# Five of twelve chunks turned by DMA through one two-part buffer, with the row statistics moved on VectorE and GpSimd, in a two-layer graph attention kernel

## What is computed

```python
def _L0_gnn_ref(xx_anchor, input, adj, weight):
    anchor_adj = jnp.einsum('md,de,ne->mn', xx_anchor, weight, input)
    scores = jnp.where(adj > 0, anchor_adj, NEG_PAD)
    atten = jax.nn.softmax(scores / TEMPERATURE, axis=1)
    return atten @ input
def _L1_gnn_ref(mole_out, adj, W, a1, a2):
    Wh = mole_out @ W
    e = jax.nn.leaky_relu((Wh @ a1)[:, None] + (Wh @ a2)[None, :], negative_slope=ALPHA)
    att = jax.nn.softmax(jnp.where(adj > 0, e, NEG_INF), axis=1)
    return jax.nn.elu(att @ Wh)
x = _layernorm(x + _L0_gnn_ref(x, L0_gnn_input, adj, L0_gnn_weight), axis=-1)
x = _layernorm(x + _L1_gnn_ref(x, adj, L1_gnn_W, L1_gnn_a1, L1_gnn_a2), axis=-1)
```

## Time and profile before

| what | value |
| --- | --- |
| median of 3 runs | 1454.98 us (1452.93 to 1455.09) |
| profiled execution, its own time | 1453.21 us |
| its span | 1451.4 us |
| mean granted TensorE clock | 0.989 |
| busy: PE, PE weight loads | 1412.1 us (97%), 1010.3 us (70%) |
| busy: DVE, ACT, POOL | 1256.5 us (87%), 1070.0 us (74%), 1215.0 us (84%) |
| DMA queue q1 | 73.1% of 16 engines' span |

### The profile page before, as it was taken

One profiled execution on the slowest core, in us unless ns is written; L12 is line 12 of the kernel. 1 busy time (PEld: TensorE's weight loads), 2 busy tenths in 40 slices (PEclk: granted clock), 3 DMA queues, 4 the chain that ended last, 5 costly groups with the idle time before them and its releaser, 6 DMA issues.

```text
span 1451.4 us, 28334 instructions
## 1 busy us (share of the span) xinstructions
PE 1412.1 (97%) x9661; PEld 1010.3 (70%) x9661; DVE 1256.5 (87%) x2129; ACT 1070.0 (74%) x2437; POOL 1215.0 (84%) x904
## 2 busy tenths in 40 slices
PE   8899999999999999999999999979999999999995
PEld 4577777777777777777777777755666666666664
DVE  6999999999999899999999999839898898979794
ACT  6788888888888888888888888868655555545453
POOL 6788888888888888888888878738999999999995
PEclk9999999999999999999999999998999999999998
DMA  8999999999999999999999999663434344434320
GB/s 265 292 270 269 262 265 257 258 275 270 270 267 263 259 264 258 273 271 271 273 258 259 262 255 274 182 138 73 102 66 111 77 102 87 102 71 105 78 58 14
DMA packets 427918, 291.38 MB, mean 201 GB/s; under 512 B 356864, under 2 KB 403200, under 8 KB 427776
## 3 DMA queue, kind: packets, MB, share of 16 engines
q1 hardware_dynamic: 427776, 289.59, 73.1%
HBM read 160.56 MB, written 40.89 MB: 139 GB/s over the span
## 4 chain that ended last, share of the span: by engine, by line
PE 94%; DVE 3%; issue 1%; ACT 1%; POOL 0%; DMA 0%; ACTq 0%; DVEq 0%; SPq 0%; POOLq 0%
PE ps L617 17%; PE ps L703 13%; PE ps L696 12%; PE ps L643 11%; PE ps L619 9%; PE ps L656 8%; PE ps L655 8%; PE ps L654 8%; PE ps L680 6%; PE ps L587 1%; PE ps L714 1%; DVE rows L969 1%; DVE neg_mask L944 1%; PE ps L580 0%; DVE pT_lo L978 0%
## 5 line engine op out<-in xcount | busy, mean ns | idle before, releaser
L826 ACT ACTIVATE rows<-rows,exp_bias 128x512 f32<-128x512 f32 x576 | 416.8, 724 | 57.0 <-DVE exp_bias L1022 57.0
L528 POOL TENSOR_TENSOR p_lo<-p,p_hi 128x1024 fp32r<-128x1024 f32 x180 | 423.7, 2394 | 22.0 <-ACT p_hi L864 11.5
L969 DVE CUSTOM_DVE_ANT_0 rows<-ps,neg_mask 128x1024 f32<-128x1024 f32 x288 | 352.1, 1223 | 80.2 <-PE ps L656 72.8
L1049 DVE SCALAR_TENSOR_TENSOR p<-ps,e_col,edgesT 128x1024 f32<-128x1024 f32 x288 | 349.7, 1275 | 53.3 <-PE ps L673 36.7
L438 POOL TENSOR_SCALAR edges<-neg_mask 128x1536 uint8<-128x1536 bf16 x190 | 307.3, 1618 | 97.0 <-DVE neg_mask L944 85.1
L864 ACT CAST p_hi<-p 128x1024 fp32r<-128x1024 f32 x180 | 185.1, 1047 | 167.0 <-DVE p L1049 164.4
L617 PE MATMUL ps<-vals,pT_hi 128*128 128x256 f16 x1536 | 295.3, 273 | 1.4 <-ACT att L805 0.9
L812 ACT CAST pT_hi<-ps 128x512 f16<-128x512 f32 x384 | 222.7, 580 | 90.6 <-PE ps L643 90.4
L480 POOL TENSOR_TENSOR inp_sb<-rows,inp_sb 128x512 f16<-128x512 f32 x192 | 281.5, 1484 | 9.6 <-ACT inp_sb L820 1.9
L619 PE MATMUL ps<-vals,pT_lo 128*128 128x128 f16 x1536 | 274.6, 219 | 0.0
L978 DVE TENSOR_TENSOR pT_lo<-ps,pT_hi 128x512 f16<-128x512 f32 x384 | 250.8, 683 | 10.6 <-ACT pT_hi L812 10.6
(11 more groups left out here) (111 smaller groups left out, 1855.9 us busy)
## 6 DMA issues: line engine op xcount, KB each, us to landing
adj_sb<-adj SPq DMA_DIRECT2D x192, 768.0 KB, 5.6
edge_rows<-edges SPq DMA_DIRECT2D x192, 192.0 KB, 4.8
xq<-x SPq DMA_DIRECT2D x48, 64.0 KB, 2.9
xr<-x SPq DMA_DIRECT2D x48, 64.0 KB, 5.6
out<-y_w SPq DMA_DIRECT2D x5, 512.0 KB, 3.7
inp_sb<-inp SPq DMA_DIRECT2D x3, 768.0 KB, 8.2
inp_sb<-inp_sb SPq DMA_TRANSPOSE x96, 4.6
edgesT<-edge_rows SPq DMA_TRANSPOSE x48, 5.3
```

The source lines that it names most:

```text
L528: nc.gpsimd.tensor_tensor(p1_lo[:, m % LO_SLOTS, :], p1[:, (NB * g + n) % P_SLOTS, :], p1_hi[:, m % HI_SLOTS, :].bitcast(F32), ALU.subtrac ...
L826: nc.scalar.activation(row_chunk(1 - par, c), row_chunk(1 - par, c), ACT.Exp, bias=exp_bias[:, 1 - par:2 - par], scale=EXP_SCALE, accum_ou ...
L969: nc.vector.tensor_tensor_reduce(row_pair(par, k), scores_pair(k), neg_mask_row[:, 2 * k * CHUNK:2 * (k + 1) * CHUNK], 1.0, -3.0e38, ALU.a ...
L1049: nc.vector.scalar_tensor_tensor(out=p1[:, (NB * g + n) % P_SLOTS, :], in0=ps[:, R_ROW:R_ROW + 2, :].rearrange("p b w -> p (b w)"), scalar ...
```

## The change

- MOVED is 5 instead of 4: a fifth chunk goes by DMA, so PE turns seven chunks per tile instead of eight. ATT_STEP is 10 instead of 9, since it is counted from MOVED.
- `movedT` is one buffer instead of two, in two parts of three and two chunks (MOVED_PARTS). SP issues four transposing DMAs per tile instead of two, and each part waits until PE has used the same part of the tile before (`pv_done`). ACT's and POOL's waits on `movedT_in` go by part.
- The row statistics of tile t - 3 now stand in iteration t on DVE, at the head of c = 2 (STATS_STEP), where they were those of tile t - 2 at c = 11. On POOL the power, normalization and `s_prod` of tile t - 3 stand behind `moved_low(t - 1, 0)` of iteration t; the two additions of tile t - 2 stay at the iteration's end. ACT's sums go to c = 9 (SUMS_STEP).
- POOL no longer keeps `x1_total`. DVE sums the first 44 tiles in eight pieces in iteration 48, and PE adds the last four in `mean_of_wh`, with one column of `averager` instead of 128.
- The last tile: DVE makes the additions, the normalization and the two row sums (with `tensor_tensor_reduce`); only the power stays on POOL.

The diff, without the renaming of PSUM places and semaphores that follow from this:

```diff
@@ before L12 @@
 PV_LAG = 2
-MOVED = 4
+MOVED = 5
+MOVED_PARTS = ((0, 3), (3, 5))
 PARTS = 8
@@ before L97 @@
 moved_hi, moved_lo = (inp_space[:, i * MW:(i + 1) * MW] for i in range(2))
-movedT = inp_space[:, 2 * MW:6 * MW].rearrange("p (s h b m) -> p s h b m", s=2, h=2, m=P)
+movedT = inp_space[:, 2 * MW:4 * MW].rearrange("p (h b m) -> p h b m", h=2, m=P)
 xq = sb0("xq", [P, P], F32)
...
@@ before L276 @@
 ATT_STEP = LAG + PV_LAG + MOVED
+STATS_STEP, SUMS_STEP = 2, 9
+TOTALLED, TOTAL_PARTS = NB - 4, 8
 
@@ before L292 @@
 def movedT_loads(tile):
-    return 32 * (tile // 2 + 1)
+    return 32 * (tile + 1)
+
+def moved_part(i):
+    return next(k for k, (a, b) in enumerate(MOVED_PARTS) if a <= i < b)
 
@@ before L375 @@
             sp.wait_ge(moved_hi_set, MOVED * (tile + 1))
-            if tile < 2:
-                sp.wait_ge(vals_lo, MOVED * (tile + 2))
-            after(sp, pv_done, C * (tile - 1))
-            sp.dma_start_transpose(movedT[:, par, 0], moved_hi).then_inc(movedT_in[par], 16)
-            sp.wait_ge(moved_lo_set, MOVED * (tile + 1))
-            sp.dma_start_transpose(movedT[:, par, 1], moved_lo).then_inc(movedT_in[par], 16)
+            if tile == 0:
+                sp.wait_ge(vals_lo, 2 * MOVED)
+            for k, (a, b) in enumerate(MOVED_PARTS):
+                after(sp, pv_done, C * (tile - 1) + (C - MOVED) + b if tile >= 1 else 0)
+                for half, of, ready in ((0, moved_hi, moved_hi_set), (1, moved_lo, moved_lo_set)):
+                    sp.wait_ge(ready, MOVED * tile + b)
+                    sp.dma_start_transpose(movedT[:, half, a * BPC:b * BPC, :], of[:, a * CHUNK:b * CHUNK]
+                                           ).then_inc(movedT_in[k], 16)
         if t == NB + 1:
@@ before L467 @@
                                 ALU.mult).then_inc(s_prod_set, 1)
-        if j == 0:
-            nc.gpsimd.tensor_copy(x1_total[:], x1).then_inc(total_set, 1)
-        else:
-            pool.wait_ge(total_set, j)
-            nc.gpsimd.tensor_tensor(x1_total[:], x1_total[:], x1, ALU.add).then_inc(total_set, 1)
 
@@ before L478 @@
         if tile >= 1:
-            pool.wait_ge(movedT_in[(tile - 1) % 2], movedT_loads(tile - 1))
+            pool.wait_ge(movedT_in[moved_part(i)], movedT_loads(tile - 1))
         nc.gpsimd.tensor_tensor(moved_lo[:, i * CHUNK:(i + 1) * CHUNK], row_chunk(tile % 2, i),
@@ before L482 @@
 
+    def rstd_of_tile(tile):
+        pool.wait_ge(ve_set, tile + 1)
+        nc.gpsimd.tensor_tensor(small[:, 4:5], small[:, 3:4], consts[:, 0:1], ALU.pow).then_inc(rstd_set, 1)
+
     def tile_rstd(t, par, known):
@@ before L489 @@
             moved_low(t - 1, 0)
+        if t >= 3:
+            tile = t - 3
+            rstd_of_tile(tile)
+            pool.wait_ge(rstd_set, tile + 1)
+            nc.gpsimd.tensor_scalar(x1_all[:, tile, :], xr[:, 1 - par, :], moments[:, 0:1], small[:, 4:5], ALU.subtract,
+                                    ALU.mult).then_inc(x1_set, 1)
+            score_cols(tile)
+        if moved:
             moved_low(t - 1, 1)
@@ before L502 @@
                 vals_low(9)
+        if moved:
+            moved_low(t - 1, 4)
+        if ahead:
             make_edges(t + 1, 1)
@@ before L506 @@
             vals_low(11)
-        if ends_tile(known):
+        if 2 <= t <= NB:
             tile = t - 2
@@ before L513 @@
             nc.gpsimd.tensor_tensor(xr[:, par, :], att[:, P:2 * P], xr[:, par, :], ALU.add).then_inc(u_set, 1)
-            pool.wait_ge(ve_set, tile + 1)
-            nc.gpsimd.tensor_tensor(small[:, 4:5], small[:, 3:4], consts[:, 0:1], ALU.pow).then_inc(rstd_set, 1)
-            pool.wait_ge(rstd_set, tile + 1)
-            nc.gpsimd.tensor_scalar(x1_all[:, tile, :], xr[:, par, :], moments[:, 0:1], small[:, 4:5], ALU.subtract,
-                                    ALU.mult).then_inc(x1_set, 1)
-            score_cols(tile)
 
     tiles(pool, tile_rstd)
+    rstd_of_tile(NB - 1)
 
...
@@ before L717 @@
     def mean_of_wh():
-        pe.wait_ge(total_set, NB)
-        nc.tensor.matmul(ps[:, SPARE, 0:P], x1_total[:], averager[:], start=True, stop=True).then_inc(mean_turned, 1)
+        pe.wait_ge(total_set, TOTAL_PARTS)
+        nc.tensor.matmul(mean_ps, x1_total[:], averager[:, 0:1], start=True, stop=False)
+        pe.wait_ge(x1_set, NB)
+        for j in range(TOTALLED, NB):
+            mm = nc.tensor.matmul(mean_ps, x1_all[:, j, :], averager[:, 0:1], start=False, stop=(j == NB - 1))
+        mm.then_inc(mean_turned, 1)
         pe.wait_ge(mean_repd, 1)
-        nc.tensor.matmul(ps[:, SPARE, P:2 * P], mean_rep[:], w1_c[:, 0:P], start=True, stop=True).then_inc(mean_made, 1)
+        nc.tensor.matmul(ps[:, OUT3, P:2 * P], mean_rep[:], w1_c[:, 0:P], start=True, stop=True).then_inc(mean_made, 1)
 
...
@@ before L830 @@
                 xT_high(t + 1, 1 - par)
-            if c == 4 and t >= 3:
+            if c == SUMS_STEP and t >= 3:
                 score_sums(t - 3)
-            if c == C - 1 and t == NB + 1:
-                score_sums(t - 2)
 
@@ before L934 @@
 
+    def row_statistics(tile):
+        dve.wait_ge(u_set, tile + 1)
+        after(dve, x1_set, tile)
+        nc.vector.bn_stats(stats[:], xr[:, tile % 2, :]).then_inc(stats_set, 1)
+        dve.wait_ge(stats_set, tile + 1)
+        nc.vector.bn_aggr(moments[:], stats[:]).then_inc(moments_set, 1)
+        dve.wait_ge(moments_set, tile + 1)
+        nc.vector.tensor_scalar(small[:, 3:4], moments[:, 1:2], EPS, None, ALU.add).then_inc(ve_set, 1)
+
     def make_mask(t, q, known):
@@ before L953 @@
         for c in range(C):
+            if c == STATS_STEP and t >= 3:
+                row_statistics(t - 3)
             if known == 0:
@@ before L980 @@
 
+            if t == NB and 1 <= c <= TOTAL_PARTS:
+                d = slice((c - 1) * P // TOTAL_PARTS, c * P // TOTAL_PARTS)
+                dve.wait_ge(x1_set, TOTALLED)
+                nc.vector.reduce_sum(x1_total[:, d], x1_all[:, 0:TOTALLED, d].rearrange("p n d -> p d n"),
+                                     AX_X).then_inc(total_set, 1)
+
             if known == 0:
@@ before L1005 @@
                                             ALU.mult).then_inc(scaled_set, 1)
-                if c == ATT_STEP + 2:
-                    dve.wait_ge(u_set, t - 1)
-                    after(dve, x1_set, t - 2)
-                    nc.vector.bn_stats(stats[:], xr[:, par, :]).then_inc(stats_set, 1)
-                    dve.wait_ge(stats_set, t - 1)
-                    nc.vector.bn_aggr(moments[:], stats[:]).then_inc(moments_set, 1)
-                if c == ATT_STEP + 2:
-                    dve.wait_ge(moments_set, t - 1)
-                    nc.vector.tensor_scalar(small[:, 3:4], moments[:, 1:2], EPS, None, ALU.add).then_inc(ve_set, 1)
+                if c == ATT_STEP + 1 and t == NB + 1:
+                    dve.wait_ge(att_out, NB)
+                    dve.wait_ge(xr_in[par], 16 * (t // 2))
+                    nc.vector.tensor_tensor(xr[:, par, :], att[:, 0:P], xr[:, par, :], ALU.add).then_inc(u1_set, 1)
+                    dve.wait_ge(u1_set, NB)
+                    nc.vector.tensor_tensor(xr[:, par, :], att[:, P:2 * P], xr[:, par, :], ALU.add).then_inc(u_set, 1)
             if c == C - 1 and scores_of(known):
@@ before L1026 @@
 
-    dve.wait_ge(s_set, NB)
+    row_statistics(NB - 1)
+    dve.wait_ge(rstd_set, NB)
+    nc.vector.tensor_scalar(x1_all[:, NB - 1, :], xr[:, (NB - 1) % 2, :], moments[:, 0:1], small[:, 4:5], ALU.subtract,
+                            ALU.mult).then_inc(x1_set, 1)
+    dve.wait_ge(x1_set, NB)
+    dve.wait_ge(s_set, NB - 1)
+    for k in range(2):
+        nc.vector.tensor_tensor_reduce(s_prod[:, k, :], x1_all[:, NB - 1, :], wa_rep[:, k, :], 1.0, 0.0, ALU.mult,
+                                       ALU.add, s_cols[:, k, NB - 1:NB]).then_inc(s_last_set, 1)
+    dve.wait_ge(s_last_set, 2)
     nc.vector.reduce_max(s_top[:, 0:1], s_cols[:, 0, :], AX_X).then_inc(s_part, 1)
...
```

18 lines of the change are left out of this document (10 added, 8 removed).

## The result

The changed kernel takes 1488.78 us (median of 4 runs, 1483.09 to 1491.58) against 1453.95 us for the kernel before, run beside it: a ratio of 1.0238, 95% interval 1.0222 to 1.0255, or +34.8 us. It is slower, as forecast, but by 23 us more than forecast, and outside the range. The profiled execution took 1489.73 us, with a span of 1487.6 us and a granted clock of 0.988.

A forecast was written before the change was run, and what follows sets the result against it. PE bounds the kernel at 19.35 us per tile; the change closes a POOL-DVE loop of 19.63 us. 1453.2 + 12.6 - 0.9 - 1.8 + 1.0 = 1464.1 us, as a median 1466 us; range 1432 to 1480 us.

The forecast's parts named there:

- The part that saves: PE: one chunk per tile fewer to turn, 0.44 us, period 19.35 to 18.91 us if PE stays the bound.
- POOL's chain and the loop: POOL's quarter-2 edges to second addition, 17.29 us, plus 2.34 us back through DVE's statistics and mask: 19.63 us per tile.
- What would show it: Signs in the trace: quarter-2 mask wait 2.2 to 2.5 us, DVE idle before statistics, PE idle 0.5 to 0.9 us.
- The hold-up of 0.74 us per mask: POOL's instructions beside DVE's masks: three masks cost POOL 2.21 us per chain, 0.74 us each.
- The single buffer and the queue of SP: SP's four transposing DMAs and the loads queued with them: cost 0, up to +0.3 us per tile.
- They are used a period later, so nothing again: SP: two adj quarters and an edge store queue behind the later xr load; costed at nothing.
- Cost 0, up to +0.3 us per tile: SP: quarter 0 of adj, issued later; if it lands 1 us late, DVE's 1.8 us free time absorbs it.
- The end of the first layer: From ACT's last att to the maximum of row sums: -1.8 us, between -1 and -2.5.
- The reductions: DVE's eight reductions in iteration 48, 0.4 to 0.9 us each: +1.0 us taken, between 0 and +5.
- PE stays the bound: Rival: the loop closes below PE's 18.91 us per tile, giving 1433 us; chance 22%.
- Every mask blocks POOL for its whole length: Rival on POOL: the loop grows 0.6 us to 20.3 us, giving 1494 us; chance 7%.
- the DMA engines become the bound: Rival: a fifth chunk's transposes take DMA work from 18.4 to 20.2 us, giving 1492 us; chance 9%.

The follow-up runs named there:

- e7: e3 with ACT's row sums at c = 11 instead of c = 9 (timing only): 1437.51 us, ratio 0.9888.
- e2: The changed kernel with quarter 3 of adj loaded in only 192 of 1536 columns from tile 1 on (timing only): 1469.62 us, ratio 1.0115.
- e10: The changed kernel with statistics at c = 3, row sums at c = 11 and xr loaded behind quarter 3 of adj: 1453.57 us, ratio 1.0003.
- e12: The changed kernel with xr loaded behind quarter 3 of adj instead of behind quarter 1: 1473.21 us, ratio 1.0139.
- e3: The changed kernel with statistics at c = 3 and quarter 3 of adj loaded in 192 of 1536 columns (timing only): 1443.96 us, ratio 0.9930.
- e11: e10 with the next tile's small load xq issued ahead of the transposing DMAs: 1444.68 us, ratio 0.9942.
- e9: e10 with quarter 0 of the next tile's adj issued ahead of the transposing DMAs: 1491.81 us, ratio 1.0253.
- e8: e4 with xr loaded behind quarter 3 of adj instead of behind quarter 1: 1454.97 us, ratio 1.0008.
- e4: The changed kernel with four chunks by DMA instead of five, parts of two and two: 1467.29 us, ratio 1.0089.

## Why the prediction was wrong in size, point by point

**The part that saves: right.** 18.91 us per tile if PE is the bound: e7 has it.

**POOL's chain and the loop: right.** 17.29 us forecast, 17.37 in the trace; way back 2.34 and 2.36; period 19.63 and 19.73. "What would show it" asked for a wait of 2.2 to 2.5 us for the quarter-2 mask (2.36) and POOL near 84% busy (16.52 of 19.73 us, 84%). Its 0.10 us too little, times 45, is 4.5 us. That the chain came so near is partly luck: its masks cost 0.26 us less than put, and its five low parts 0.37 us more, since one that stands by itself takes up to 1.25 us to the next start and not 1.12. The statistics' idle time released by the second addition was to be there in nearly every tile; it is in 26 of 43 tiles (100 to 960 us), and in 43 once the load is light (e2): in the others `adj` had already delayed DVE.

**The hold-up of 0.74 us per mask: near, 0.65.** In the chain shown above it falls on a low part (1.75 against 1.16), the normalization (1.57 against 0.80) and an edge conversion (2.06 against 1.47): 1.95 us for three, 0.65 each. The Trainium skill's rule (SBUF — State Buffer, Who interferes with whom), that a 2-port VectorE instruction which is issued first blocks GpSimd for its whole length, would have made it 0.95 us each and the tile 20.3 us, by the rival that I drew from it; in steady tiles the trace doesn't agree in size, as POOL lost 0.59 to 0.77 us and the tile takes 19.73. The power on one column loses the same, 0.77 us: it takes 1.33 us in some tiles, 0.56 in others. In kind the trace agrees: in e10, as shown, whichever of mask and edge conversion starts first keeps its length and the other is held, the mask by 1.1 us.

**The single buffer and the queue of SP: this step failed.** "They are used a period later, so nothing again" looked at the quarters that queue behind `xr` and asked only whether they themselves would be late. They weren't. But by leaving 5 to 6 us late they are in flight beside the transposing DMAs. The "issues of some 2 us each" were right as a median (2.14 us); four of them hold SP for a median of 8.6 us, up to 10.1, where it is 7.1 with `xr` late (e12). Behind them `xq` and quarter 0 wait.

Two things failed in the treatment of quarter 0. The room was too small: the prediction had it issued 18.4 us into POOL's chain and wanted at 23.9 us, 5.5 us apart; in the tile shown it was issued at 18.8 us (523.97 - 505.15) and wanted at 23.4 us (528.57), 4.6 us apart, with a median of 4.4 us against a landing of 5.0. And that DVE's free time of 1.8 us "takes it up" was wrong: the time free per period is not free at a place on the loop. ACT's wait for the transposing DMAs and PE's for `xq` were put at nothing as well. "Cost 0, up to +0.3 us per tile": measured 20.21 - 19.73 = 0.48 us per tile as a mean, 21 us in all, of which `xr` alone is some 15 us (e12).

**The row sums at c = 9: not costed.** 0.19 us per tile where PE is the bound (e3 to e7), hidden behind the loop in the change as it stands.

**The end of the first layer: right, -1.9 for -1.8. The reductions: +0.8 for +1.0, by luck.** Each was put at 0.4 to 0.9 us and took 1.33 to 1.39, so 10.9 us of DVE's time went in and the `att` moved by 0.8. The second layer's +1.2 us was put at next to nothing; no run takes it apart.

The sum with the measured sizes: 45 x (19.73 - 19.35) - 0.9 - 1.9 + 0.8 + 1.2 = +16.3 us, beside +15.3 measured without the late loads (e2), and +21 for these: +37.3, beside 1489.73 - 1453.21 = +36.5 us between the profiled executions.

**The rivals.** "PE stays the bound" needed a loop under 18.91; it isn't. "Every mask blocks POOL for its whole length" and "the DMA engines become the bound" gave 1494 and 1492 us, near the result, by mechanisms that the runs don't bear out as put: no steady 20.2 or 20.3 us per tile, but 29 periods of 44 at the loop's 19.5 to 19.9 and the rest late in steps, and with another order on SP the same five chunks run at 18.91 in most tiles (e10, e11). The second was the nearer one, as the place is right: DVE waiting for `adj` before its masks was its sign, and it came. I gave it 9%. What I should have done is to price a partial form of it, a tile in three that is 1 to 3 us late. That the total fell near these two rivals' prices says nothing for their mechanisms.

**What stays open.** Why the load of some tiles lands a few tenths of a us later than that of their neighbours; where the step of 2.2 us comes from (that of 1.25 us goes with the order of mask and edge conversion in e10, untested by a run of its own); why `xq` ahead helped; and whether the slow transposing DMAs are held by the issuing side or by the engines that move the data. No run takes these apart. Two quarters of `adj` ahead of the transposing DMAs weren't tried, once one had cost what it did in e9.

## What to carry to other kernels

When a step moves the thing that a load in an ordered queue waits for, look at everything behind it in the queue, and ask not only whether it lands in time but what it will be in flight beside. An engine's free time per period is worth nothing at a place that lies on a loop through another engine: close the loop on paper, then add every wait that can fall on it. And a fifth chunk by DMA paid only once statistics, row sums and two small loads stood in the right places; the change and e11, the same code in two orders, are 44 us apart.

## What the runs showed of the hardware

In the two tiles of e10 shown, the one of mask (VectorE) and edge conversion (GpSimd) that started first kept its length, and the other was held: 0.94 us for the mask and 2.15 for the conversion in one order, 2.08 and 1.47 in the other.

A transposing DMA holds the engine that issues it far longer than a plain one, and by an amount that depends on what is in flight: a median of 0.43 us for a load of a quarter of `adj` (in the kernel before and in the change), against a median of 1.3 us for two chunks beside at most one quarter in flight (e8), 1.5 us beside two (e4), and in the change, where half of them turn three chunks, 2.1 us, with 4.5 at most:

```profile
L390 SPq DMA_TRANSPOSE inp_sb<-inp_sb x157: 1254/2140/4515, 109.0 to 899.3; - x157
...
DMA to landing us min/median/max: 3.2/4.9/8.2
```

With the same sizes and `xr` late (e12) the median is 1.60 us, and 4.2 us to landing.

The Trainium skill (Perfetto Trace Analysis, DMA Instruction — HWDGE) says that such a row spans the wait for the descriptor generator, the making of all descriptors and the engine's own semaphore increments, and not the moving of the data. The traces agree: the landing lies beyond the row's end (a median of 4.9 us against 2.1). The row itself grew with more in flight, by 0.2 us between e8 and e4.

Packet time can pass the span: over the 800 us the share of 1.02 goes with 268 GB/s, where 0.94 went with 266, and in the period of the tile on the loop it is 1.05 with 268. e10 moved 281 GB/s at the same 1.02. So a share of 1.02 was no limit in bytes; packets took longer for the same bytes.
